# A ViT block on one core: values weighed in three fp16 passes, with the exps' terms cast in halves

## The chip, the cores and the metric

The kernel runs on one core of a Trainium2 chip. The metric is the device time of one execution in microseconds (us), the median of three runs. TensorE does matmuls (PE in the profile, its weight loads PEld), VectorE is DVE, ScalarE ACT, GpSimd POOL; SyncE (SP) issues the DMAs.

## The reference, cut to what matters

Eight batches of 512 tokens go through a tokenizer product, an attention block with 16 heads of 16 columns and a mixture of eight experts with sigmoid gates:

```python
h = einsum('bhid,oi,od->bho', x, weighted_sum, weight)      # [8, 512, 256]
h = h + attn(layernorm(h)); h = h + ffn(layernorm(h))
# attn: qkv = tokens @ qkv_w.T + qkv_b; q, k rotated and scaled to unit length
scores = einsum('bhqd,bhkd->bhqk', q, k) * 16 ** -0.5
out = einsum('bhqk,bhkd->bhqd', softmax(scores), v)         # then @ out_w.T + out_b
# ffn, for each of 8 experts: relu(x @ W1[e] + b1[e]) @ W2[e] + b2[e], times its gate, all summed
```

## The kernel before, in words

Everything is in fp32 quality; where matmuls are fp16, both operands are split in a high and a low fp16 half and three products are summed (high x high, high x low, low x high).

The FFN of one batch is 64 chunks, 8 for each expert. A chunk's first step (`f1`) is 6 matmuls into `bank_h`, then on ScalarE two Relus (`h32` in fp32 and `hh`, the high half, L724 and L727), then on GpSimd the low half `hl` (L616). Three chunks later comes its second step (`f2`), 12 matmuls into `bank_f`; after 8 chunks VectorE adds the expert's result (`acc`, L1150).

The attention of batch b+1 runs between the FFN chunks of batch b. `attention_order` gives each attention step a place, in chunks from the FFN's start, and `merge` writes one list of all steps. Every engine walks that same list, and each does its own part of a step, with semaphores between them; so the list sets the order on all engines. ScalarE alone first passes the list through `exps_first`, which swaps an `f1` with a `scores` step that directly follows it, so that the exp comes ahead of the chunk's Relus:

```python
for k in range(len(order) - 1):
    if order[k][0] == "f1" and order[k + 1][0] == "scores":
        order[k], order[k + 1] = order[k + 1], order[k]
```

A scores phase has 16 units (`UNITS`: 4 groups of heads x 4 tiles of keys) of two halves. Half n is a step `scores n`, `PACE` = 0.66 chunk after the one before, from 25.6 on: two row-tiled fp16 matmuls of 512 columns into `bank_s` (L820), then on ScalarE one exp of 128x1024 into `probs` (L693). There is one pair of score banks, so `scores n` waits on TensorE for exp n-1. The step `weigh u`, three paces after the unit's first scores, multiplies the unit's four heads with the values `v1` into `bank_o`: four fp32 matmuls in four column tiles of 32 (L834; the profile records two a matmul). `v1` has for each head 16 columns of values and 16 of ones, which give the sum of the exps. `probs` has two buffers, so an exp of unit u waits for the weighing of unit u-2. After four units come `out_copy` and `out_turn` (transposes, a reciprocal and a product, L1073 and L1076), and after all of them the projection, the second layernorm, the gates (`gates_turn`, L884, and a copy on ScalarE) and the bias matmuls (`bias2`, L891).

Batch 0's attention has no FFN beside it. Beside batch 0's FFN run batch 1's attention and the preparation of the experts: for each, VectorE takes maxima of the raw weights (`maxima`, L1163), computes scales (`scales`, L1194 to L1210) after a DMA round trip, and splits the weights in halves in four parts (`parts`: the high half on ScalarE, L739, the low on VectorE, L1174). In batches 1 to 7 the FFN loads the split weights from memory.

A `qkv` step adds the bias into `qk` and `v1` on VectorE (L1025, L1026); `rotate` then uses `tmp_b`, `tmp_a` (GpSimd, L623) and ScalarE's squares.

## Time and profile before

| | us |
|---|---|
| median of 3 runs | 1947.99 (1947.15 to 1950.42) |
| the profiled execution, its span | 1948.63, 1946.8 |
| TensorE busy | 1840.2 (95%) |
| ScalarE busy | 1070.7 (55%) |
| VectorE busy | 753.6 (39%) |
| GpSimd busy | 661.6 (34%) |

The profile is of one execution. Busy is the union of an engine's instructions; start-to-start times are shorter than durations, as neighbours overlap by some 0.1 us. "Idle before" names the engine that ended the wait. The mean granted TensorE clock is 0.98 of full speed; it is lower in parts of the first 130 us and around 200 to 250 us.

### The profile page before, as it was taken

Reading aid. Unit: us, or ns where it says so; the run is one execution under the profiler, and the core shown is the slowest. Engines: PE = TensorE matmul, PEld = TensorE weight load, DVE = VectorE, ACT = ScalarE, POOL = GpSimd, SP = SyncE. Lnnn points to the kernel's source line nnn. Section 1 sums busy time; section 2 is a strip of 40 time slices with the busy share of each in tenths; the row PEclk is TensorE's granted clock in tenths of the full one; section 3 lists DMA queues with packets and bytes.
Section 4 is the critical chain, followed back from the end, with each engine's and each line's share of the span. In section 5 each row is a group of like instructions: output and inputs, shape, how many; then the busy total and the mean of one; then the engine's idle time right before and its main releaser. Section 6 shows DMA issues by size and latency. Waiting matters only on the chain.

```text
span 1946.8 us, 31769 instructions
## 1 busy us (share of the span) xinstructions
PE 1840.2 (95%) x12608; PEld 1163.8 (60%) x12608; DVE 753.6 (39%) x1600; ACT 1070.7 (55%) x1645; POOL 661.6 (34%) x559
## 2 busy tenths in 40 slices
PE   5469799999999999999999999999999999999999
PEld 4137444676457754677546764577645775466666
DVE  7866744546014540246213470044601454021001
ACT  2544477545764466554665456644565546655444
POOL 1003422334233342334323343233423334234443
PEclk9689899999999999999999999999999999999999
DMA  4421543434123151231513333133412314122221
GB/s 161 130 98 39 149 144 132 159 120 109 65 81 128 64 130 66 87 120 66 130 66 109 98 91 105 63 112 98 124 52 106 114 66 114 65 87 98 109 91 52
DMA packets 109780, 194.55 MB, mean 100 GB/s; under 512 B 72616, under 2 KB 86464, under 8 KB 93248
## 3 DMA queue, kind: packets, MB, share of 16 engines
q1 hardware_dynamic: 109632, 192.51, 30.6%
q8 instruction: 100, 1.64, 0.3%
q14 instruction: 48, 0.39, 0.1%
HBM read 154.73 MB, written 20.98 MB: 90 GB/s over the span
## 4 chain that ended last, share of the span: by engine, by line
PE 77%; DVE 8%; DMA 4%; ACT 3%; issue 3%; SPq 0%; DVEq 0%; ACTq 0%
PE bank_h L908 28%; PE bank_f L927 10%; PE bank_f L930 9%; PE bank_f L929 9%; PE bank_o L834 5%; PE bank_s L820 4%; PE bank_s L750 3%; PE bank_s L751 3%; PE bank_s L752 3%; DMA kt<-probs 1%; DMA kt<-stack 1%; DVE tmp_b L1038 1%; DVE acc L1150 1%; DMA raw<-in_w_dram 1%; DVE y L948 1%
## 5 line engine op out<-in xcount | busy, mean ns | idle before, releaser
L616 POOL TENSOR_TENSOR hl<-h,hh 128x512 f16<-128x512 f32 x512 | 600.4, 1173 | 1159.6 <-ACT hh L727 722.7
L908 PE MATMUL bank_h<-x,w1s 128*128 128x512 f16 x3072 | 752.5, 382 | 7.6 <-ACT hh L727 7.2
L724 ACT ACTIVATE h<-bank_h,b1s 128x512 f32<-128x512 f32 x512 | 351.3, 686 | 467.0 <-PE bank_h L908 466.9
L927 PE MATMUL bank_f<-w2s,hh 128*128 128x256 f16 x2048 | 561.4, 274 | 14.2 <-DVE acc L1150 14.2
L929 PE MATMUL bank_f<-w2s,hh 128*128 128x256 f16 x2048 | 559.6, 273 | 0.0
L930 PE MATMUL bank_f<-w2s,hl 128*128 128x256 f16 x2048 | 559.5, 273 | 0.0
L908 PEld LDWEIGHTS bank_h<-x,w1s 128*128 128x128 f16 x3072 | 287.8, 99 | 335.5 <-issue 45.6
L727 ACT ACTIVATE hh<-bank_h,b1s 128x512 f16<-128x512 f32 x512 | 350.0, 684 | 0.0
L693 ACT ACTIVATE probs<-bank_s 128x1024 f32<-128x1024 f32 x240 | 246.5, 1027 | 175.3 <-PE bank_s L820 174.2
L927 PEld LDWEIGHTS bank_f<-w2s,hh 128*128 128x128 f16 x2048 | 201.7, 98 | 123.2 <-issue 58.0
L1150 DVE SCALAR_TENSOR_TENSOR acc<-bank_f,gw,acc 128x256 f32<-128x256 f32 x256 | 106.1, 477 | 367.8 <-PE bank_f L930 367.5
L929 PEld LDWEIGHTS bank_f<-w2s,hh 128*128 128x128 f16 x2048 | 201.0, 98 | 50.8 <-issue 0.2
L930 PEld LDWEIGHTS bank_f<-w2s,hl 128*128 128x128 f16 x2048 | 200.9, 98 | 23.8
L1073 DVE RECIPROCAL rc<-bank_m 128x16 f32<-128x16 f32 x32 | 8.2, 257 | 379.1 <-PE bank_m L844 379.1
L834 PE MATMUL bank_o<-probs,v 128*32 128x512 f32 x1024 | 138.1, 612 | 1.0 <-ACT tmp_b L648 0.6
L820 PE MATMUL bank_s<-qt,kt 64*128 64x512 f16 x480 | 94.7, 391 | 35.7 <-DMA kt<-probs 25.8
L820 PEld LDWEIGHTS bank_s<-qt,kt 64*128 64x128 f16 x480 | 23.2, 93 | 120.5 <-issue 78.4
L750 PE MATMUL bank_s<-mix,xh 128*128 128x256 f32 x240 | 71.6, 298 | 16.6 <-DVE xl L971 16.6
L971 DVE TENSOR_TENSOR xl<-xraw,xh 128x512 fp32r<-128x512 f32 x58 | 41.9, 732 | 76.1 <-ACT xh L648 63.0
L752 PE MATMUL bank_s<-mix,xl 128*128 128x256 f32 x240 | 68.5, 285 | 0.0
L751 PE MATMUL bank_s<-mix,xh 128*128 128x256 f32 x240 | 68.3, 284 | 0.0
L623 POOL TENSOR_TENSOR tmp_a<-qk,cos 128x512 f32<-128x512 f32 x32 | 40.8, 1276 | 78.2 <-DVE qk L1025 78.2
(157 smaller groups left out, 1520.0 us busy)
## 6 DMA issues: line engine op xcount, KB each, us to landing
w1s<-w_parts SPq DMA_DIRECT2D x56, 1024.0 KB, 4.8
w2s<-w_parts SPq DMA_DIRECT2D x56, 1024.0 KB, 4.8
raw<-in_w_dram SPq DMA_DIRECT2D x16, 1024.0 KB, 6.6
xraw<-in_x_t_dram SPq DMA_DIRECT2D x30, 512.0 KB, 4.8
w_parts<-w1s SPq DMA_DIRECT2D x8, 1024.0 KB, 8.7
w_parts<-w2s SPq DMA_DIRECT2D x8, 1024.0 KB, 11.4
out_dram<-acc SPq DMA_DIRECT2D x16, 256.0 KB, 6.0
turned_gates<-maxima_rows SPq DMA_DIRECT2D x6, 192.0 KB, 3.5
```

What stands on the lines that cost most here:

```text
L616: pool.tensor_tensor(hl[n % HBUFS][:], h32[n % 2][:], hh[n % HBUFS][:], ALU.subtract)\
L693: act.activation(probs[u % 2][:, 2 * half:2 * half + 2, :], score_banks(n, fb is None)[:, :, :], ACT.Exp, scale=SCORE_SCALE).then_inc(expe ...
L724: act.activation(h32[n % 2][:], bank_h[n % 2][:, :], ACT.Relu, bias=b1s[:, e, m:m + 1]).then_inc(h_hi.sem, 1)
L727: act.activation(hh[n % HBUFS][:], bank_h[n % 2][:, :], ACT.Relu, bias=b1s[:, e, m:m + 1]).then_inc(h_hi.sem, 1)
L750: pe.matmul(out_ap, high[k], w[k], start=start and k == 0, stop=False, skip_group_check=True)
L752: last = pe.matmul(out_ap, low[k], w[k], start=False, stop=stop and k == n - 1, skip_group_check=True)
L820: pe.matmul(score_banks(n, fb is None)[:, j, :], kt[lo:lo + 64, h // 2, tile * P:(tile + 1) * P], qt[lo:lo + 64, h // 2, :], start=True, s ...
L834: last = pe.matmul(bank_o[32 * j:32 * j + 32, :], v1[:, tile, h, :, :].rearrange("p s d -> p (s d)"), probs[n % 2][:, j, :], start=(tile = ...
L908: last = pe.matmul(bank_h[n % 2][:, :], w[:, wp, k, m * P:(m + 1) * P], x16s[fb % 2][:, xp, k, :], start=(k == 0 and wp + xp == 0), stop=( ...
L927: pe.matmul(o, high, w[:, 0, m, :], start=(m == 0 and t % 2 == 0), stop=False, skip_group_check=True)
L929: pe.matmul(o, high, w[:, 1, m, :], start=False, stop=False, skip_group_check=True)
L930: last = pe.matmul(o, low, w[:, 0, m, :], start=False, stop=(m == HM - 1), skip_group_check=True)
```

## The change

Batch 0's attention is computed as before. From batch 1 on:

- The values are kept in fp16 as a high and a low half (`v16`, in the bytes of the old `v1`, which is now `v32`). A weighing is three passes of four column-tiled fp16 matmuls (v high x p high, v low x p high, v high x p low) instead of one of fp32.
- The exps write fp32 terms into `exps`, two buffers in `qk`, which is free by then, and wait only for the subtraction that last read that buffer. A new step `halves n`, 0.8 pace behind `scores n`, casts them into halves in the bytes of `probs`: the high half of even n on ScalarE right behind the exp, that of odd n on VectorE, the low half of both by a subtraction on VectorE. These casts wait for the weighing of unit u-2.
- `weigh` comes one pace later (four paces after its unit's first scores), and with it `out_copy`, `out_turn` and everything behind (`behind` = 1).
- On `qkv`, v goes through `tmp_b`: bias added, cast, subtraction; the rotation waits for that.
- Once, the largest value of v's weights is found (`v_max`: a VectorE reduction and a GpSimd reduction across partitions), and after batch 0's attention VectorE scales the v part of `qkvw` and `qkvb` by a power of two and `outw` back (`v_scaled`; GpSimd writes the ones and zeros of `v16`).

```diff
-    first = 25.6
+    first, behind = 25.6, 0 if alone else 1
     for n in range(2 * UNITS):
-        steps.append((first + PACE * n, "scores", n))
+        steps += [(first + PACE * n, "scores", n), (first + PACE * (n + 0.8), "halves", n)]
     for u in range(UNITS):
-        steps.append((first + PACE * min(2 * u + 3, 2 * UNITS) + 1e-6, "weigh", u))
+        steps.append((first + PACE * min(2 * u + 3 + behind, 2 * UNITS + behind) + 1e-6, "weigh", u))
...
-    prep = []
+    prep = [(3.4, "v_scaled", 0)]
...
+        halves = [p[:].rearrange("p j t -> p (j t)").bitcast(F16).rearrange("p (s j t) -> p s j t", s=2, j=4)
+                  for p in probs]
+        exps = [qk[:, 2 * i:2 * i + 2, :] for i in range(2)]
...
                 elif stage == "scores":
                     u, half = divmod(n, 2)
-                    if half == 0:
+                    if half == 0 and ab == 0:
                         wait(act, weighed, ab, u - 1)
                     wait(act, scored, ab, 2 * n + 2)
+                    if ab == 0:
+                        terms = probs[u % 2][:, 2 * half:2 * half + 2, :]
+                    else:
+                        wait(act, qk_unit, ab, TT)
+                        wait(act, halved, ab - 1, n - 1)
+                        terms = exps[n % 2]
+                    act.activation(terms, score_banks(n, fb is None)[:, :, :], ACT.Exp, scale=SCORE_SCALE)\
+                       .then_inc(exped.sem, 1)
+                    if ab and half == 0:
+                        wait(act, exped, ab, n + 1)
+                        wait(act, weighed, ab, u - 1)
+                        copy(halves[u % 2][:, 0, 0:2, :], terms).then_inc(high_even.sem, 1)
...
                 elif stage == "weigh":
                     g, tile = divmod(n, TT)
...
+                    if ab == 0:
+                        passes = [(v32[:, tile], probs[n % 2])]
+                    else:
+                        v_high, v_low = v16[:, 0, tile], v16[:, 1, tile]
+                        p_high, p_low = halves[n % 2][:, 0], halves[n % 2][:, 1]
+                        passes = [(v_high, p_high), (v_low, p_high), (v_high, p_low)]
+                    for k, (v, p) in enumerate(passes):
+                        for j in range(4):
+                            last = pe.matmul(bank_o[32 * j:32 * j + 32, :],
+                                             v[:, 4 * g + j].rearrange("p s d -> p (s d)"), p[:, j, :],
+                                             start=(tile == 0 and k == 0),
+                                             stop=(tile == TT - 1 and k == len(passes) - 1), skip_group_check=True)
...
+                    values = tmp_b[:, 0:D]
+                    wait(dve, summed, ab, n)
+                    half_v.link(dve, dve.tensor_tensor(values, at_v[:, 0:D], qkvb[:, 2 * D:QKV], ALU.add))
+                    values = values.rearrange("p (h d) -> p h d", d=HD)
+                    half_v.link(dve, dve.tensor_copy(v16[:, 0, n, :, 0, :], values))
+                    dve.tensor_tensor(v16[:, 1, n, :, 0, :], values, v16[:, 0, n, :, 0, :], ALU.subtract)\
+                       .then_inc(qkv_out.sem, 1)
...
+                elif stage == "halves":
+                    u, half = divmod(n, 2)
+                    high, low = (halves[u % 2][:, part, 2 * half:2 * half + 2, :] for part in range(2))
+                    wait(dve, weighed, ab, u - 1)
+                    if half:
+                        wait(dve, exped, ab, n + 1)
+                        half_v.link(dve, dve.tensor_copy(high, exps[n % 2]))
+                    else:
+                        wait(dve, high_even, ab - 1, u + 1)
+                    dve.tensor_tensor(low, exps[n % 2], high, ALU.subtract).then_inc(halved.sem, 1)
```

ScalarE, from the first scores of batch 2 on, before (an exp is `probs<-bank_s`, a chunk's Relus are `h` and `hh`):

```order
L693 ACTIVATE probs<-bank_s 128x1024 x2
L724 ACTIVATE h_0<-bank_h,b1s 128x512
L727 ACTIVATE hh<-bank_h,b1s 128x512
L693 ACTIVATE probs<-bank_s 128x1024
L724 ACTIVATE h_1<-bank_h,b1s 128x512
L727 ACTIVATE hh<-bank_h,b1s 128x512
L693 ACTIVATE probs<-bank_s 128x1024 x2
```

The same place now (an exp is `qk<-bank_s`, the cast of an even half `probs<-qk`):

```order
L721 ACTIVATE qk<-bank_s 128x1024
L670 ACTIVATE probs<-qk 128x1024
L756 ACTIVATE h_0<-bank_h,b1s 128x512
L759 ACTIVATE hh<-bank_h,b1s 128x512
L721 ACTIVATE qk<-bank_s 128x1024 x2
L670 ACTIVATE probs<-qk 128x1024
L756 ACTIVATE h_1<-bank_h,b1s 128x512
L759 ACTIVATE hh<-bank_h,b1s 128x512
L721 ACTIVATE qk<-bank_s 128x1024
L756 ACTIVATE h_0<-bank_h,b1s 128x512
L759 ACTIVATE hh<-bank_h,b1s 128x512
L721 ACTIVATE qk<-bank_s 128x1024
```

The second exp stood ahead of the first chunk's Relus and now stands behind them; so does the fifth, which was one of a pair.

VectorE in batch 1's scores, from one pair of scale computations on, before (`scl`, `unscale`, `b1s` end a scale computation, `w1s`, `w2s` are parts, `mx` maxima):

```order
L1207 TENSOR_SCALAR scl<-inv 128x2
L1208 SCALAR_TENSOR_TENSOR unscale<-pow 128x1
L1210 TENSOR_SCALAR b1s<-b1raw,scl 128x8
L1174 SCALAR_TENSOR_TENSOR w1s<-raw,scl,w1s 128x1024 x2
L1174 SCALAR_TENSOR_TENSOR w2s<-raw,scl,w2s 128x1024
L1073 RECIPROCAL rc<-bank_m 128x16
L1076 TENSOR_TENSOR normed<-bank_m,rc 128x4x64
L1174 SCALAR_TENSOR_TENSOR w2s<-raw,scl,w2s 128x1024
```

The same place now (`probs<-qk` casts, `probs<-qk,probs` subtractions):

```order
L1303 TENSOR_SCALAR b1s<-b1raw,scl 128x8
L1133 CAST probs<-qk 128x1024
L1136 TENSOR_TENSOR probs<-qk,probs 128x1024
L1243 SCALAR_TENSOR_TENSOR w1s<-raw,scl,w1s 128x1024
L1136 TENSOR_TENSOR probs<-qk,probs 128x1024
L1243 SCALAR_TENSOR_TENSOR w1s<-raw,scl,w1s 128x1024
L1133 CAST probs<-qk 128x1024
L1136 TENSOR_TENSOR probs<-qk,probs 128x1024
L1243 SCALAR_TENSOR_TENSOR w2s<-raw,scl,w2s 128x1024
L1136 TENSOR_TENSOR probs<-qk,probs 128x1024
L1243 SCALAR_TENSOR_TENSOR w2s<-raw,scl,w2s 128x1024
```

Between the parts of an expert there is now a halves step each.

TensorE at the gates of batch 1, before (`wg` the gates' transposes, `b2sb` the bias matmuls):

```order
L884 MATMUL bank_m<-ident,wg 24x128 x4
L927 MATMUL bank_f<-w2s,hh 128x256
L929 MATMUL bank_f<-w2s,hh 128x256
L930 MATMUL bank_f<-w2s,hl 128x256
```

There the twelve matmuls of an f2 chunk follow, and then the bias matmuls. Now:

```order
L972 MATMUL bank_f<-w2s,hh 128x256
L974 MATMUL bank_f<-w2s,hh 128x256
L975 MATMUL bank_f<-w2s,hl 128x256
L929 MATMUL bank_m<-ident,wg 24x128 x4
L936 MATMUL bank_s<-b2sb,turned_gates 128x256 x4
```

The f2 chunk stands ahead of both, and the bias matmuls come directly behind the transposes.

## Rows read from the trace of the kernel before

**Rows 1.** The page: busy time by engine; the chain that ended last.
```profile
PE 1840.2 (95%) x12608; PEld 1163.8 (60%) x12608; DVE 753.6 (39%) x1600; ACT 1070.7 (55%) x1645; POOL 661.6 (34%) x559
...
PE 77%; DVE 8%; DMA 4%; ACT 3%; issue 3%; SPq 0%; DVEq 0%; ACTq 0%
```

**Rows 2.** Busy us (instructions) by engine, TensorE clock, DMA, in two windows.
```profile
240.00:335.00 95.00, 90.04 (x588) 42.39 (x589) 40.92 (x67) 70.08 (x89) 24.33 (x21) 0.97 0.42 139
...
710.00:805.00 95.00, 95.00 (x645) 47.28 (x644) 7.03 (x18) 63.70 (x87) 32.08 (x27) 1.00 0.24 79
```

**Rows 3.** Timeline, TensorE, batch 3's scores: start us, us, engine, line, what, count.
```profile
715.07 0.39 PE L820 MATMUL bank_s<-qt,kt 64*128 64x512 f16 x2
...
748.51 0.16 PEld L834 LDWEIGHTS bank_o<-probs,v 128*32 128x32 f32 x8 [0.23 <-issue]
...
748.51 1.07 PE L834 MATMUL bank_o<-probs,v 128*32 128x512 f32 x8
...
749.51 0.28 PE L927 MATMUL bank_f<-w2s,hh 128*128 128x256 f16 x1
...
750.92 0.39 PE L820 MATMUL bank_s<-qt,kt 64*128 64x512 f16 x2
...
751.25 1.47 PE L908 MATMUL bank_h<-x,w1s 128*128 128x512 f16 x6
...
752.55 0.27 PE L927 MATMUL bank_f<-w2s,hh 128*128 128x256 f16 x1
...
799.77 0.64 PE L834 MATMUL bank_o<-probs,v 128*32 128x512 f32 x4
```

**Rows 4.** Timeline, ScalarE, the same stretch.
```profile
749.57 0.68 ACT L724 ACTIVATE h<-bank_h,b1s 128x512 f32<-128x512 f32 x1
...
750.14 0.69 ACT L727 ACTIVATE hh<-bank_h,b1s 128x512 f16<-128x512 f32 x1
...
751.44 1.02 ACT L693 ACTIVATE probs<-bank_s 128x1024 f32<-128x1024 f32 x1 [0.61 <-PE bank_s L820]
...
752.75 0.69 ACT L724 ACTIVATE h<-bank_h,b1s 128x512 f32<-128x512 f32 x1 [0.29 <-PE bank_h L908]
```

**Rows 5.** ScalarE by line and shape: count | busy us, mean ns | idle before.
```profile
L648 ACT ACTIVATE mix<-probs 128x1024 fp32r<-128x1024 f32 x2 | 2.1, 1056 | 7.2 <-DVE probs L464 7.2
```

**Rows 6.** VectorE by line and shape.
```profile
L1174 DVE SCALAR_TENSOR_TENSOR w1s<-raw,scl,w1s 128x1024 f16<-128x1024 f32 x16 | 20.5, 1282 | 18.2 <-ACT w1s L739 18.0
...
L1172 DVE TENSOR_SCALAR w1s<-raw,scl 128x1024 f16<-128x1024 f32 x4 | 3.0, 748 | 0.0
...
L1076 DVE TENSOR_TENSOR normed<-bank_m,rc 128x256 f32<-128x256 f32 x32 | 13.6, 424 | 1.1
```

**Rows 7.** Timeline, VectorE and GpSimd, batch 3's rotations.
```profile
674.44 0.69 DVE L1043 TENSOR_TENSOR qk<-tmp_a,tmp_b 128x512 f32<-128x512 f32 x1
...
680.67 1.16 POOL L616 TENSOR_TENSOR hl<-h,hh 128x512 f16<-128x512 f32 x1 [0.61 <-PE bank_f L930]
...
680.71 1.66 DVE L1043 TENSOR_TENSOR qk<-tmp_a,tmp_b 128x512 f32<-128x512 f32 x1
```

**Rows 8.** Timeline, TensorE, three places.
```profile
135.47 0.57 PE L891 MATMUL bank_s<-b2sb,turned_gates 24*128 24x256 f32 x1 [0.68 <-ACT turned_gates L648]
...
332.71 0.64 PE L834 MATMUL bank_o<-probs,v 128*32 128x512 f32 x4
...
695.57 0.27 PE L927 MATMUL bank_f<-w2s,hh 128*128 128x256 f16 x1 [1.14 <-DVE acc L1150]
```

**Rows 9.** Timeline, VectorE, start of batch 1's scores.
```profile
245.25 2.29 DVE L1163 TENSOR_REDUCE mx<-raw 128x1 f32<-128x2048 f32 x1 [9.06 <-DMA raw<-in_w_dram]
...
247.72 1.66 DVE L1150 SCALAR_TENSOR_TENSOR acc<-bank_f,gw,acc 128x256 f32<-128x256 f32 x4
...
255.67 0.68 DVE L1194 TENSOR_REDUCE mxr<-turned_gates 128x3 f32<-128x384 f32 x1 [6.30 <-DMA turned_gates<-maxima_rows]
...
257.97 0.23 DVE L1210 TENSOR_SCALAR b1s<-b1raw,scl 128x8 f32<-128x8 f32 x1
```

More of the change, by code:

```diff
@@ L131, in merge @@
         return order
-    between = {("scores", 0): [("maxima", 0), ("maxima", 1), ("reduce", 0), ("scales", 0),
+    between = {("scores", 0): [("v_max", 0), ("maxima", 0), ("maxima", 1), ("reduce", 0), ("scales", 0),
                                ("parts", 0), ("parts", 1), ("parts", 2), ("parts", 3)],
@@ L140, in bodies @@
     first = []
-    for step in attention_order(alone=True):
+    for step in [s for s in attention_order(alone=True) if s[1] != "halves"]:
         first += [step[1:]] + between.get(step[1:], [])
@@ L823, in steps @@
                     g, tile = divmod(n, TT)
-                    wait(pe, exped, ab, 2 * (n + 1))
+                    if ab == 0:
+                        wait(pe, exped, ab, 2 * (n + 1))
+                    else:
+                        wait(pe, halved, ab - 1, 2 * (n + 1))
+                    if n == 0 and ab == 1:
+                        pe.wait_ge(pool_consts, 2)
                     if n == 0:
@@ L831, in steps @@
                         wait(pe, o_out, ab, g)
-                    for j in range(4):
-                        h = 4 * g + j
-                        last = pe.matmul(bank_o[32 * j:32 * j + 32, :],
-                                         v1[:, tile, h, :, :].rearrange("p s d -> p (s d)"),
-                                         probs[n % 2][:, j, :], start=(tile == 0), stop=(tile == TT - 1),
-                                         skip_group_check=True)
+                    if ab == 0:
+                        passes = [(v32[:, tile], probs[n % 2])]
[9 more added lines that the diff above has]
+                                             stop=(tile == TT - 1 and k == len(passes) - 1), skip_group_check=True)
                     last.then_inc(weighed.sem, 1)
@@ L1174, in steps, with scale_values @@
                     dve.scalar_tensor_tensor(low, cut, scale, high, ALU.mult, ALU.subtract).then_inc(parts_lo, 1)
+            def scale_values():
+                link = scale_v.link
+                b_v = qkvb[:, 2 * D:QKV]
+                dve.wait_ge(v_max_all, 1)
+                dve.tensor_reduce(vbound[:, 1:2], b_v, AX.X, ALU.max, apply_absolute_value=True)
+                link(dve, dve.tensor_tensor(vbound[:, 0:1], vmxr[:, 0:1], vmxr[:, 1:2], ALU.max))
+                link(dve, dve.scalar_tensor_tensor(vbound[:, 0:1], vbound[:, 0:1], float(D), vbound[:, 1:2],
+                                                   ALU.mult, ALU.add))
+                link(dve, dve.tensor_scalar(vbound[:, 0:1], vbound[:, 0:1], FLOOR, None, ALU.max))
+                link(dve, dve.tensor_scalar(vbound[:, 0:1].bitcast(I32), vbound[:, 0:1].bitcast(I32), EXPONENT, None,
+                                            ALU.bitwise_and))
+                link(dve, dve.tensor_scalar(vbound[:, 1:2].bitcast(I32), vbound[:, 0:1].bitcast(I32), -1.0,
+                                            float(2 * ONE_BITS), ALU.mult, ALU.add))
+                dve.tensor_scalar(vscl[:, 1:2], vbound[:, 0:1], 1.0 / TOP, None, ALU.mult)
+                link(dve, dve.tensor_scalar(vscl[:, 0:1], vbound[:, 1:2], TOP, None, ALU.mult))
+                wait(dve, projected, 0, TT)
+                for part in range(2):
+                    w_v, w_o = qkvw[:, part, :, 2 * D:QKV], outw[:, part]
+                    dve.tensor_scalar(w_v, w_v.bitcast(F32), vscl[:, 0:1], None, ALU.mult)
+                    dve.tensor_scalar(w_o, w_o.bitcast(F32), vscl[:, 1:2], None, ALU.mult)
+                dve.tensor_scalar(b_v, b_v, vscl[:, 0:1], None, ALU.mult).then_inc(v_scaled, 1)
+                dve.wait_ge(v_scaled, 1)
             def stack_b2():
```

47 lines of the change are left out of this document (37 added, 10 removed).

## The prediction

> **What bounds the kernel now.** I read the page first, then busy times by window, then one scores stretch as a timeline of TensorE and of ScalarE, then VectorE in the stretch where expert weights are still being split. The page shows TensorE busy 95% of the span and 77% of the chain that ended last; the other engines are busy 34 to 55% [rows 1]. By window the kernel has two kinds of scores phase (32 score steps and 16 weighings of one batch, beside the FFN of the batch before). In batches 2 to 7 TensorE has no idle time (95.00 of 95 us), VectorE works 7 us of 95 and ScalarE 64. In batch 1, whose scores run beside the FFN of batch 0, VectorE already works 41 us of 95, since it splits the raw weights there, and ScalarE 70 [rows 2]. So an operation on VectorE is nearly free in six phases and dear in one.
>
> **The weighing.** One weighing holds TensorE 1.00 us, from its start to that of the next instruction, 748.51 to 749.51 [rows 3]; the records are eight, two for each fp32 matmul, four column tiles at a time. The change makes it three fp16 passes of four tiles in the 112 weighings of batches 1 to 7. No row shows a 32-column fp16 pass. Nearest: six FFN matmuls of 512 fp16 columns followed by an FFN matmul of another kind take 1.30 us (751.25 to 752.55), so 0.22 each; a score step, one pass of two row tiles, takes 0.33 (750.92 to 751.25), so a change of tiling adds about 0.11 [rows 3]. That gives 0.11 + 3 x 0.22 = 0.77; if each pass stood alone, 3 x 0.33 = 0.99; if the change of tiling overlapped by a third, 0.73. I take 0.78, near the first, since the fp32 row has the same four tiles overlapping. Gain: 0.22 us a weighing, 3.5 a batch, 24.6 in all; bounds 1 and 30.
>
> The loads of the second four tiles are done by 748.67 (0.16 us from 748.51) while the first four still compute [rows 3]. The Trainium skill, TensorE: Matmul & The Clock Gate, section Part 3 (packing small matmuls), has it that weight loads overlap running matmuls only where the row group differs, and column tiles share theirs. By that rule each pass would show its load and the weighing would cost about the 0.99 above, leaving a gain of 1 us in place of 24.6; the row is against it.
>
> **ScalarE in the scores phase.** It gains one copy of 128x1024 to fp16 for each even half. A row of that size from SBUF is 1.06 us [rows 5], about 0.95 from start to start. The copy waits for the end of its own exp, so an even half costs 1.02 + 0.04 + 0.95 = 2.0 us where it was 0.92. The FFN's two Relus of a chunk occupy 1.14 (749.57 to 750.14 is one, 0.57) [rows 4]. Per unit (two halves, 1.32 chunks): 2.0 + 0.92 + 1.5 + 0.12 for the output copy = 4.5 us, against TensorE's two score steps, a weighing, 1.32 chunks of 1.30 + 1.35 and its share of the output transposes: 0.64 + 0.78 + 3.50 + 0.13 = 5.0. It fits, with little room, and here the order matters. Before, exps_first swaps an exp ahead of the Relus of the chunk just before it. The new "halves" step stands between "f1" and "scores" in the list, so most swaps no longer happen: the exp is now queued behind Relus whose matmuls end only as its own scores start. TensorE's next score step needs that exp, since there is one pair of score banks.
>
> I walked the phase with these figures (exp 0.51 us after its scores start, Relus 1.50 after their matmuls start, an f2 chunk before a score step 1.41, an f1 chunk 1.40 [rows 3, 4]). One stretch of it, in us from score step 8: step 12 stands at 11.07, its exp at 11.58 to 12.60, the copy to 13.58. TensorE goes on with the weighing, the output transposes and f1 of chunk 34 at 12.67, so the Relus run from 14.17 to 15.31. Step 13 comes at 14.07; its exp is ready at 14.58 but runs from 15.31 to 16.33. Step 14 would come 0.32 + 1.41 after step 13, at 15.80, and starts at 16.38. Over the phase TensorE stalls before score step 2 (1.3 us), 8 (0.6), 14 (0.6), 18 (0.1), 20 (0.6) and 24 (0.5): 3.7 us. Before there was none: the 85.7 us from step 0 to the end of weighing 15 (715.07 to 799.77, and 1.0) [rows 3] are what the pieces add up to. So the 3.5 us are given back, +0.2 a batch. The last weighing now needs VectorE's last cast and subtraction 3.7 us after its scores; +0.1.
>
> **VectorE in batches 2 to 7.** Each unit gains two subtractions of 128x1024 with two SBUF inputs and one cast. Nearest rows: L1174, some 1.28 us, and L1172, 0.75 [rows 6]; 3.3 us of 5.0, where little else runs. But an instruction with two SBUF inputs waits while GpSimd runs: the 0.69 us L1043 took 1.66 when a GpSimd subtraction had started 0.04 us ahead of it [rows 7]. The halves have a pace (2.4 us) to spare before the exp that reuses their buffer, which covers one such wait; I cost it at 0, and as a rival below.
>
> **Smaller places, once a batch.** (a) All attention steps behind the weighing come one pace (0.66 chunk) later. That takes away the f2 chunk between the transposes of the gates and the bias matmuls. In batch 0 they already stand side by side: 0.68 us idle on top of the transposes [rows 8]. The TensorE clock is full here in the later batches (1.00 in the scores window [rows 2]); I take 0.8, for the copy and its latencies. (b) With v, VectorE gains a cast and a subtraction of 256 columns before each rotation (0.6 to 0.8 us together, a quarter of rows 6 and a start each). After tile 3 its queue is unbroken up to the acc of expert 1, for which TensorE already waits 1.1 us [rows 8]; 0 to 0.85 of it comes through, partly absorbed by GpSimd's turns; I take 0.4. Sum with the 0.3 above: 1.5 us a batch.
>
> **VectorE in batch 1.** Between the first and the last halves step its list holds 3 accs (1.7 each), 3 scale computations (2.5, 255.67 to 258.2), 11 subtractions of weight parts (1.28), 2 pairs of maxima (4.6), 3 output turns (0.42 and a reciprocal, 0.7) by [rows 6, 9]: 37.9 us. The halves add 32 x 1.28 + 16 x 0.78 = 53.4. Together 91.3. The first halves step stands behind the maxima that end at 247.5, after a 9.06 us wait for a DMA [rows 9]. 247.5 + 91.3 = 338.8, with VectorE never idle. The last weighing ended at 333.7 before (332.71 [rows 8] and 1.0), and 1.4 us of FFN that came after it now come ahead: 335.1. So at least +4 us. On top: each part waits for ScalarE's copy, which is now queued behind exps that wait for halves; by a walk of one expert's period about 1 us a period, 3 in all; and 59 instructions take the port that GpSimd holds a quarter of the time (24.3 of 95 us [rows 2]), 0.15 us each, 9 in all. +16, bounds +4 and +27 (0.3 us a conflict, 6 us of waits). Scores, exps and weighings follow VectorE and TensorE is in order, so all of this lands on the end.
>
> **The rest.** Scaling v's weights is some 12 VectorE instructions, 4 to 5 us by the durations of rows 6 and 9, near the start of batch 1's steps, where VectorE still waits for other engines and a DMA; 0 to 3 us of it can come through, I take 1. The maximum of the v weights (0.7 us) and the two GpSimd memsets lie where those engines wait: 0.
>
> **Sum.** Seven batches x 1.5 for the once-a-batch places and the phase's balance, without the 0.2 + 0.1 in batch 1 which the +16 replaces: 6 x 1.5 + 1.2 = 10.2. With 16 and 1: +27.2. Before, the profiled execution took 1948.6 us (span 1946.8), the median 1948.0; so 1976.
>
> **Rivals.**
> Other side, faster (23%): TensorE stays the sole bound in batches 2 to 7, because a score step finds its exp done in spite of the lost swaps. The deciding point is ScalarE's backlog when an exp becomes ready: below 0.2 us at the short gaps (0.32 + 1.41 us) there is no stall. For it: ScalarE has 31 us free in 95 [rows 2] and needs 15. Against: the exp behind two Relus has 1.14 us of backlog by construction. Then 6 x (-3.5 + 1.3) = -13.2, batch 1 at its minimum +4 + 1.2 + 1: -7, so 1942; with 0.73 for the weighing 5 less, 1937.
> VectorE keeps up in batch 1 (12%): its DMA and ScalarE waits of before are all filled, no port conflicts show, +4; the stalls stay. 1948.6 + 10.2 + 5 = 1964.
> The port decides everywhere (13%): 3.3 us of VectorE and 1.32 x 1.16 of GpSimd are 4.8 us a unit of 5.0; if they exclude each other wholly and an exp waits one more GpSimd instruction every fourth unit, that is 4 x 1.2 us a batch: 1976 + 29 = 2005. For it: rows 7. Against: both have slack of a pace or a chunk.
> The change not doing what it says (fp16 passes that cost 0.99): 1976 + 6 x 1 at most, since the stalls shrink as the weighing grows; inside the range, no own chance.
>
> The Trainium skill, FP8 and Floating Point Precision, section TensorE Precision Notes, has fp32 as four passes through the array, so that three fp16 passes would be three quarters of it: 112 weighings of 1.00 us x 1/4 = 28 us less by that estimate, against my 24.6. As a rule for the whole kernel it gives 1921, which holds only if nothing but TensorE counts; I give that 2% within the faster rival, since rows 2 show the other engines' load.
>
> **How the numbers follow.** My forecast has 52%, the rivals 23, 12 and 13. Likeliest time 1976, its own range 1960 to 1990. Eight times in ten: 1940 to 1996, which leaves out the far ends of the faster rival and most of the port's. Within 0.2% (3.9 us, about what a measurement of this kernel can tell) is reached only between cases: 4%. Faster 24%, slower 72%.
>
> **What would show it.** In the changed profile: the weighing near 0.78 us from start to next; TensorE idle before scores released by ScalarE's exps, 3 to 4 us a batch in batches 2 to 7; the last weighing of batch 1 some 15 us later than the 332.71 of before [rows 8], with VectorE above 90% busy ahead of it; the bias matmuls released by ScalarE's copy, 7 times some 0.8 us; VectorE's subtractions mostly at 1.28 with some above 2. Wrong would be: scores phases of batches 2 to 7 some 3 us shorter than the 85.7 from step 0 to the end of weighing 15 [rows 3], or batch 1 with VectorE idle while TensorE works.

## The result, and the profile after

The changed kernel takes 1970.55 us (median of 4 runs, 1969.12 to 1971.10) against 1947.70 us before (4 runs, 1947.15 to 1950.42): ratio 1.0108, 95% interval 1.0096 to 1.0121. It is slower by 1.1%. The profiled execution has a span of 1967.2 us, 20.4 more than before.

The page of the changed kernel, busy time by engine and the chain that ended last; both answer to [rows 1]:

```profile
PE 1823.4 (93%) x13056; PEld 1173.3 (60%) x13056; DVE 1144.3 (58%) x2006; ACT 1182.5 (60%) x1757; POOL 710.4 (36%) x562
...
PE 69%; DVE 10%; ACT 6%; issue 5%; DMA 4%; SPq 0%; ACTq 0%; DVEq 0%
```

TensorE has less to do and a smaller share of the chain; VectorE's busy time rose by 391 us. Where the time went shows in the starts of the f1 chunks, which cut the execution into the periods of the eight FFNs. The first f1 matmul of FFN 0 started at 125.14 us before and starts at 124.88 now; that of FFN 1 started at 395.94 and starts at 410.33:

```profile
124.88 0.59 PE L953 MATMUL bank_h<-x,w1s 128*128 128x512 f16 x1
...
410.33 0.38 PE L953 MATMUL bank_h<-x,w1s 128*128 128x512 f16 x1
```

So FFN 0's period, which carries batch 1's attention, went from 270.80 to 285.45 us (+14.65). Cut the same way, the periods of FFNs 1 to 6 sum to 1379.98 before and 1385.98 now (+1.0 each), FFN 7 has 170.89 and 170.88, and the start is 0.26 earlier. That is the 20.4. FFN 0's 14.65 in turn are 3.37 ahead of batch 1's first score step (118.46 where it was 115.09), 8.93 from the first to the last score step (98.69, was 89.76) and 2.35 behind it (68.30, was 65.96).

The windows that answer to [rows 2] (us, then busy us and instructions of TensorE, its weight loads, VectorE, ScalarE, GpSimd, granted clock, DMA share, GB/s), one in batch 1's scores and one in batch 3's:

```profile
243.00:343.00 100.00, 84.15 (x616) 42.71 (x617) 86.04 (x110) 83.05 (x101) 28.26 (x20) 0.97 0.37 122
725.50:820.50 95.00, 91.60 (x706) 48.21 (x707) 59.07 (x66) 79.59 (x102) 38.83 (x27) 1.00 0.25 81
```

TensorE, which had no idle time in batch 3, now has 3.4 us; in batch 1 VectorE is busy 86 of 100 us where it was 41 of 95. What TensorE waits for over the whole kernel (us in total, times, longest):

```profile
PE bank_s L854 <- ACT qk L721: 31.1, 42, 2.4
...
PE bank_s L936 <- ACT turned_gates L670: 5.4, 8, 0.7
...
PE bank_s L782 <- DVE v L1084: 3.3, 2, 2.7
...
PE bank_o L879 <- DVE probs L1136: 2.8, 1, 2.8
```

L854 are the scores, L936 the bias matmuls, L782 the qkv matmuls, L879 the weighing. The first row was 4.5 us before, the second one place of 0.7.

**The weighing.** A timeline of the changed kernel, one weighing of batch 3, TensorE's loads (PEld) and matmuls:

```profile
740.76 0.34 PEld L879 LDWEIGHTS bank_o<-probs,v 128*32 128x32 f16 x12 [0.23 <-issue]
740.76 0.83 PE L879 MATMUL bank_o<-probs,v 128*32 128x512 f16 x12
...
741.52 0.28 PE L972 MATMUL bank_f<-w2s,hh 128*128 128x256 f16 x1
```

From its start to the next instruction it takes 0.764 us (median of 96 in batches 2 to 7) where it took 0.998. The twelve loads are done in 0.34 us beneath the matmuls. The Trainium skill, TensorE: Matmul & The Clock Gate, Part 3 (packing small matmuls), lets loads overlap running matmuls only where the row group differs; the 0.99 that the prediction worked out for that case did not come.

**The steady phase.** Batch 3's first and last score step of the changed kernel, and its one long stall, on TensorE's timeline:

```profile
730.99 0.39 PE L854 MATMUL bank_s<-qt,kt 64*128 64x512 f16 x2
...
732.72 0.39 PE L854 MATMUL bank_s<-qt,kt 64*128 64x512 f16 x2
...
735.68 0.39 PE L854 MATMUL bank_s<-qt,kt 64*128 64x512 f16 x2 [1.16 <-ACT qk L721]
...
813.34 0.39 PE L854 MATMUL bank_s<-qt,kt 64*128 64x512 f16 x2
```

82.35 us from first to last score step, where it was 81.97 (715.07 in [rows 3], and 797.04 for the last). Inside lie 14 weighings, so 14 x 0.234 = 3.3 us less work; 78.7 would be left, and 3.65 are lost. TensorE's waits before score steps add up to 3.2 of them; the other 0.4 is not accounted for. ScalarE's timeline of the same moment shows how:

```profile
732.51 1.06 ACT L670 ACTIVATE probs<-qk 128x1024 f16<-128x1024 f32 x1
733.47 0.67 ACT L756 ACTIVATE h<-bank_h,b1s 128x512 f32<-128x512 f32 x1
734.04 0.68 ACT L759 ACTIVATE hh<-bank_h,b1s 128x512 f16<-128x512 f32 x1
734.61 1.02 ACT L721 ACTIVATE qk<-bank_s 128x1024 f32<-128x1024 f32 x1
```

The exp of score step 1 (scores at 732.72) starts only at 734.61, behind the copy of the even half and both Relus, and TensorE's step 2 waits for it.

**Batch 1.** VectorE by line, from its first low half to the end of the phase (count | busy us, mean ns | idle before and its releaser):

```profile
L1136 DVE TENSOR_TENSOR probs<-qk,probs 128x1024 f16<-128x1024 f32 x31 | 40.2, 1311 | 0.5
...
L1133 DVE CAST probs<-qk 128x1024 f16<-128x1024 f32 x15 | 10.8, 718 | 1.6 <-ACT qk L721 1.6
L1243 DVE SCALAR_TENSOR_TENSOR w1s<-raw,scl,w1s 128x1024 f16<-128x1024 f32 x6 | 7.8, 1304 | 3.1 <-ACT w1s L771 3.1
L1243 DVE SCALAR_TENSOR_TENSOR w2s<-raw,scl,w2s 128x1024 f16<-128x1024 f32 x5 | 6.7, 1337 | 1.7 <-ACT w2s L771 1.7
```

And the last weighing of batch 1 on TensorE's timeline, which answers to the 332.71 of [rows 8]:

```profile
348.77 0.60 PE L879 MATMUL bank_o<-probs,v 128*32 128x512 f16 x5 [2.77 <-DVE probs L1136]
```

It is 16.1 us later and waits for VectorE.

The 3.37 us ahead of the scores are not waits of TensorE. From FFN 0's first f1 to batch 1's first score step, before and now:

```profile
125.14:240.23 115.09, 94.13 (x594) 64.47 (x595) 80.61 (x146) 53.74 (x86) 40.64 (x31) 0.92 0.29 78
```

```profile
124.88:243.34 118.46, 97.49 (x593) 66.36 (x594) 87.72 (x167) 53.88 (x86) 43.39 (x33) 0.90 0.28 76
```

The idle time is 21.0 us in both; TensorE is busy 3.36 us longer with the same work, at a lower mean granted clock (0.90 for 0.92). One such stretch is new. TensorE waits 2.7 us for the halves of v, and then the granted clock is at its lower level (1.2 GHz) for 3.4 us; before, the wait at that place was 1.2 us, and the clock stayed full (1.00 in 190 to 194). Its timeline and the window behind the wait:

```profile
190.35 0.76 PE L782 MATMUL bank_s<-qkvw,turned_h 128*128 128x512 f32 x1 [2.70 <-DVE v L1084]
```

```profile
190.30:193.70 3.40, 3.35 (x10) 2.80 (x11) 3.37 (x5) 1.07 (x3) 1.58 (x1) 0.51 0.00 0
```

### The profile page after: what moved, and what is told of

Read it like the earlier page. It is cut to its first block, busy times and chain, and to the rows that moved or that the text cites. A ratio compares the mean times of both kernels' runs of the same rounds, so it can differ in the third digit from the quotient of the medians.

```text
span 1967.2 us, 33635 instructions
## 1 busy us (share of the span) xinstructions
PE 1823.4 (93%) x13056; PEld 1173.3 (60%) x13056; DVE 1144.3 (58%) x2006; ACT 1182.5 (60%) x1757; POOL 710.4 (36%) x562
## 4 chain that ended last, share of the span: by engine, by line
PE 69%; DVE 10%; ACT 6%; issue 5%; DMA 4%; SPq 0%; ACTq 0%; DVEq 0%
PE bank_h L953 26%; PE bank_f L972 9%; PE bank_f L974 8%; PE bank_f L975 8%; PE bank_o L879 3%; PE bank_s L782 3%; ACT qk L721 3%; PE bank_s L783 3%; PE bank_s L784 3%; PE bank_s L854 3%; ACT hh L759 1%; DVE probs L1136 1%; DMA kt<-stack 1%; DMA kt<-probs 1%; DVE acc L1217 1%
## 5 line engine op out<-in xcount | busy, mean ns | idle before, releaser
L631 POOL TENSOR_TENSOR hl<-h,hh 128x512 f16<-128x512 f32 x512 | 646.7, 1263 | 1131.0 <-ACT hh L759 688.1
L1136 DVE TENSOR_TENSOR probs<-qk,probs 128x1024 f16<-128x1024 f32 x224 | 276.9, 1240 | 126.3 <-ACT probs L670 122.2
L759 ACT ACTIVATE hh<-bank_h,b1s 128x512 f16<-128x512 f32 x512 | 348.7, 681 | 0.0
L721 ACT ACTIVATE qk<-bank_s 128x1024 f32<-128x1024 f32 x224 | 229.3, 1024 | 64.1 <-PE bank_s L854 52.5
L854 PE MATMUL bank_s<-qt,kt 64*128 64x512 f16 x480 | 94.2, 389 | 60.4 <-ACT qk L721 31.1
L1133 DVE CAST probs<-qk 128x1024 f16<-128x1024 f32 x112 | 94.3, 842 | 56.3 <-ACT qk L721 56.3
L670 ACT ACTIVATE probs<-qk 128x1024 f16<-128x1024 f32 x112 | 118.4, 1057 | 3.6
L879 PE MATMUL bank_o<-probs,v 128*32 128x512 f16 (+1 forms) x1472 | 111.7, 406 | 3.8 <-DVE probs L1136 2.8
L854 PEld LDWEIGHTS bank_s<-qt,kt 64*128 64x128 f16 x480 | 23.0, 92 | 145.6 <-ACT qk L721 71.0
L782 PE MATMUL bank_s<-mix,xh 128*128 128x256 f32 x240 | 71.6, 298 | 16.7 <-DVE xl L1016 16.6
```

The lines of the kernel that those rows point to most:

```text
L631: pool.tensor_tensor(hl[n % HBUFS][:], h32[n % 2][:], hh[n % HBUFS][:], ALU.subtract)\
L721: act.activation(terms, score_banks(n, fb is None)[:, :, :], ACT.Exp, scale=SCORE_SCALE)\
L759: act.activation(hh[n % HBUFS][:], bank_h[n % 2][:, :], ACT.Relu, bias=b1s[:, e, m:m + 1]).then_inc(h_hi.sem, 1)
L782: pe.matmul(out_ap, high[k], w[k], start=start and k == 0, stop=False, skip_group_check=True)
L854: pe.matmul(score_banks(n, fb is None)[:, j, :], kt[lo:lo + 64, h // 2, tile * P:(tile + 1) * P], qt[lo:lo + 64, h // 2, :], start=True, s ...
L879: last = pe.matmul(bank_o[32 * j:32 * j + 32, :], v[:, 4 * g + j].rearrange("p s d -> p (s d)"), p[:, j, :], start=(tile == 0 and k == 0), ...
```

## The experiments

All are made from the changed kernel and named as in their expectations (e1, e2, ...). Durations called a phase run from a batch's first score step to its last. A ratio is to runs of the kernel before, taken beside that experiment (medians 1947.98 to 1948.64).

**e1: exps ahead of the Relus again.**

```diff
 def exps_first(order):
-    order = list(order)
+    order = [step for step in order if step[0] != "halves"]
```

> ScalarE's list looks past the halves steps, so that an exp again runs ahead of the Relus of the chunk that precedes it; nothing else changes. Theory (an exp waits behind two Relus): TensorE's idle time before scores in batches 2 to 7 (31.1 us in the whole changed kernel, of which 12.2 in batch 1 and 4.5 in batch 0 were there or have another cause) goes to below 0.5 us a batch, and each of the six batches gets 3 to 4 us shorter: 1970.5 - 6 x 3.5 = 1949.5, so no different from the kernel before. Batch 1 moves by less than 2 us, since VectorE sets it. Rival (TensorE's wait comes from something else, such as the even halves' copy alone or VectorE's halves): 1968 to 1971, and the idle time before scores stays at 3 us a batch. Second rival (the Relus are now late and f2 waits for them): the idle time moves to the FFN matmuls, 1960 or more.

Measured: 1958.46 us (5 runs), ratio to before 1.0051 (1.0039 to 1.0064), 12 us less than the changed kernel where 21 were expected. TensorE's timeline, batch 3, first and last score step:

```profile
729.29 0.39 PE L854 MATMUL bank_s<-qt,kt 64*128 64x512 f16 x2
...
809.78 0.39 PE L854 MATMUL bank_s<-qt,kt 64*128 64x512 f16 x2
```

80.49 us, 1.85 less. ScalarE's timeline there: the exp of step 1 now comes ahead of the Relus, but still behind the copy.

```profile
730.80 1.06 ACT L670 ACTIVATE probs<-qk 128x1024 f16<-128x1024 f32 x1
731.77 1.01 ACT L721 ACTIVATE qk<-bank_s 128x1024 f32<-128x1024 f32 x1
732.67 0.68 ACT L756 ACTIVATE h<-bank_h,b1s 128x512 f32<-128x512 f32 x1
```

The lost swaps are shown as half of the 3.65 us. The first theory named them as the whole; 1.8 us stayed, 1.4 of it in short waits before score steps 4 (0.52), 18 (0.41), 24 (0.41) and 30 (0.09). The periods of FFNs 1 to 6 are 10.5 us shorter in sum, and FFN 0's is 2.0 shorter.

**e8: all casts of halves on VectorE in batches 2 to 7, on top of e1.**

```diff
-                    if ab and half == 0:
+                    if ab == 1 and half == 0:
...
-                    if half:
+                    if half or ab > 1:
                         wait(dve, exped, ab, n + 1)
```

> As e1_swap, and in batches 2 to 7 VectorE also casts the even halves, so that ScalarE has no copy left in the scores steps there. In e1_swap the stretch from the first to the last score step was still 80.49 us, 1.8 above what its pieces add up to (81.97 of before less 14 weighings x 0.234 = 78.7). Theory (the rest is ScalarE's copy of the even half, 0.96 us from start to start, which stands ahead of the next exp): 78.7, so 6 x 1.8 = 10.8 less than the 1958.5 of e1_swap: 1947.6. Rival (VectorE now has some 4.2 us of casts and subtractions in a unit of 5.0 and stays behind, above all where GpSimd holds it up, so that exps wait for halves): 80.5 or more, 1958 to 1970.

Measured: 1953.88 us (11 runs), ratio 1.0027 (1.0018 to 1.0036), 4.6 us less than e1 where 10.8 were expected. Batch 3's phase on TensorE's timeline, and the window of [rows 2]:

```profile
727.57 0.39 PE L854 MATMUL bank_s<-qt,kt 64*128 64x512 f16 x2
...
807.36 0.39 PE L854 MATMUL bank_s<-qt,kt 64*128 64x512 f16 x2
```

```profile
725.50:820.50 95.00, 94.21 (x728) 50.25 (x727) 81.52 (x84) 63.46 (x87) 34.54 (x27) 1.00 0.23 80
```

79.79 us: the copy accounts for 0.7 of the 1.8. Of the last 1.1 us, 0.8 are TensorE's waits before score steps 4, 5, 8 and 18; 0.3 is not accounted for. Before steps 4, 5 and 8 (0.7 us) the exp that the step needs had itself waited for VectorE, which is busy 81.5 of 95 us now. Ten of the phase's 32 exps wait for it, as the rival had said. The lines show GpSimd, VectorE and ScalarE:

```profile
740.17 1.16 POOL L631 TENSOR_TENSOR hl<-h,hh 128x512 f16<-128x512 f32 x1 [4.18 <-ACT hh L759]
740.31 2.11 DVE L1136 TENSOR_TENSOR probs<-qk,probs 128x1024 f16<-128x1024 f32 x1
...
745.37 1.02 ACT L721 ACTIVATE qk<-bank_s 128x1024 f32<-128x1024 f32 x1 [1.81 <-DVE probs L1136]
```

A low half that starts while a GpSimd instruction runs takes 2.10 us in the mean (84 of the 192 in batches 2 to 7), any other 1.23 at most. In the changed kernel none of the 192 took more than 1.23.

**e4: a fourth pass in the weighing.**

```diff
+                        if ab > 1:
+                            passes.append((v_low, p_low))
```

> The weighing gets a fourth fp16 pass (low half of v by low half of the exps) in batches 2 to 7: 96 times a pass of some 0.22 us, 20.9 us of TensorE's work, 14 of 16 in a batch between its first and last score step. Theory (that stretch holds 3.6 us of idle time in which TensorE waits for ScalarE's exps, and a longer weighing moves the next score step later and so fills it): the stretch of 82.35 us grows by 0 to 1 us, the two weighings behind it by 0.4: +3 to +9 us, 1973 to 1979. Rival (TensorE is the bound and every us of it counts): +20.9, 1991.

Measured: 1988.33 us (4 runs), 17.8 more than the changed kernel, where 3 to 9 were expected and 20.9 by the rival. The theory fell. What TensorE waits for in batch 3's phase, first in the changed kernel, then in this one:

```profile
PE bank_s L854 <- ACT qk L721: 3.2, 5, 1.2
```

```profile
PE bank_s L854 <- ACT qk L721: 2.9, 5, 1.1
```

A weighing takes 0.980 us (0.216 for the pass); the phase grew by 2.7 of 14 x 0.216 = 3.0 us, and the waits are the same five. The order on TensorE's timeline says why: before score step 2 no weighing has run yet, and before steps 8, 14 and 20 the weighing stands ahead of the f1 chunk whose Relus the exp waits behind. There a longer weighing moves the Relus and the exp by the same amount as the score step that waits, and the waits are 0.53 us in both kernels. Only before step 24 does the wait shrink, from 0.41 to 0.18. A wait that a queue order makes is not slack.

**e3: bias matmuls one f2 chunk later.**

```diff
             else:
-                while waiting:
+                while waiting and waiting[0][0] < c + 0.5:
                     order.append(waiting.pop(0)[1:])
```

> The bias matmuls stand one f2 chunk (1.3 us) later in every batch with an FFN beside it; the transposes of the gates stay. Theory: TensorE's wait of 0.68 us for ScalarE's copy of the transposed gates goes in seven places, 7 x 0.7 = 4.9: 1965.6. Rival (the next thing is late instead: the first mix of the coming batch or the first f1 needs VectorE's bias additions, now 1.3 us later): no gain, 1970 to 1971, with a new wait of 0.5 us or more behind the bias matmuls.

Measured: 1964.93 us (median of 5 runs; four lie between 1964.24 and 1966.12, and one took 3704.04, for which nothing on record has a cause), 5.6 less than the changed kernel, where 4.9 were expected. From the last score step to the next FFN's first f1 batches 2 to 7 take 59.38 us instead of 60.13, six times 0.75; batch 1, where more varies, takes 67.07 instead of 68.30. No wait before the bias matmuls is left in batches 1 to 7.

**e6: batch 1 as before.** The fp32 weighing, its buffers and its order are kept for batch 1; `v_scaled` moves to the first steps of batch 2.

```diff
-                    if ab == 0:
+                    if ab < 2:
                         passes = [(v32[:, tile], probs[n % 2])]
...
-    return first, merge(attention + prep, done=2), merge(attention), merge([])
+    return (first, merge(kept + prep, done=2), merge(attention + [(3.4, "v_scaled", 0)]), merge(attention),
+            merge([]))
```

> Batch 1 keeps the fp32 weighing and its order of before; the three fp16 passes start with batch 2, and the scaling of v's weights moves to the start of batch 2's steps. Theory: the FFN period of batch 0, 14.65 us longer after the change, goes back to what it was, less 0 to 1 us for the maxima; batch 2's period gains 0.3 to 1 us for the scaling: 1970.5 - 14 = 1956.5 (1955 to 1958). Rival (part of the 14.65 us is carried in from the stretches before, so that it stays): 1960 or more. Second rival (the scaling costs as much in batch 2, since TensorE has no idle time there to hide it): 1959 to 1961.

Measured: 1953.03 us (8 runs), ratio 1.0026 (1.0016 to 1.0036), 17.5 less than the changed kernel where 14 were expected. FFN 0's period is 270.62 us (126.35 to 396.97), what it was before, and batch 2's is no longer than in the changed kernel (230.76 against 231.11), so the scaling of v's weights costs nothing there. The granted clock in 190 to 194 is 1.00 again. By the spans the gain is 15.1 us, of which 14.8 is this period; the medians show 2.4 more, which lies within their spread. Batch 1 is three quarters of the loss.

**What sets batch 1's pace: VectorE relieved, both relieved, ScalarE relieved.** Three kernels, in batch 1 alone: e2, the subtraction of the low half on 8 of 512 columns; e9, that and the even halves cast on VectorE instead of ScalarE; e11, ScalarE's copy on 8 of 512 columns.

```diff
-                        passes = [(v_high, p_high), (v_low, p_high), (v_high, p_low)]
+                        passes = [(v_high, p_high), (v_low, p_high), (v_high, p_high if ab == 1 else p_low)]
...
-                    dve.tensor_tensor(low, exps[n % 2], high, ALU.subtract).then_inc(halved.sem, 1)
+                    cut = 8 if ab == 1 else TOKENS
+                    dve.tensor_tensor(low[:, :, 0:cut], exps[n % 2][:, :, 0:cut], high[:, :, 0:cut], ALU.subtract)\
+                       .then_inc(halved.sem, 1)
```

> In batch 1 alone VectorE's subtraction of the low half of the exps covers 8 of 512 columns (about 0.1 us for 1.31), and the third pass of the weighing reads the high half, so TensorE's work is the same and the low half of batch 1's exps is left out of the result. Theory (VectorE sets the pace of batch 1's scores): 32 x 1.2 = 38 us of VectorE's time go, and the scores phase of batch 1, 98.7 us from the first score step to the last, gets back to the 90 us of before less what the steady batches show, so 7 to 10 us less: 1961 to 1963. Rival (batch 1 is slowed by ScalarE, whose copies of weight parts, exps and even halves queue up): less than 3 us less, 1968 to 1970.

```diff
-                    if ab and half == 0:
+                    if ab > 1 and half == 0:
...
-                    if half:
+                    if half or ab == 1:
                         wait(dve, exped, ab, n + 1)
...
```

> As e2_low_sliver (batch 1 subtracts 8 columns of 512 and leaves the low half of its exps out), and in batch 1 VectorE instead of ScalarE casts the even halves. In e2_low_sliver the stretch from first to last score step of batch 1 was still 95.85 us, where TensorE's work is 89.76 - 3.3 = 86.5. Theory (with VectorE relieved, ScalarE is the next bound there: exps, copies of even halves, Relus and copies of weight parts; 16 x 0.96 = 15.4 us of its queue go): the stretch falls by 4 to 8 us to 88 to 92, the kernel to 1956 to 1960. Rival (the rest is the order of the exps behind Relus and weight parts alone, or VectorE's scale computations and maxima): less than 2 us, 1962 to 1964.

```diff
-                        copy(halves[u % 2][:, 0, 0:2, :], terms).then_inc(high_even.sem, 1)
+                        cut = 8 if ab == 1 else TOKENS
+                        copy(halves[u % 2][:, 0, 0:2, 0:cut], terms[:, :, 0:cut]).then_inc(high_even.sem, 1)
...
+                        if ab == 1:
+                            p_high, p_low = (part[:, 2:4] for part in (p_high, p_low))
...
```

> In batch 1 alone ScalarE's copy of the even half covers 8 of 512 columns, VectorE's subtraction for it takes the exps on both sides (same size), and the weighing reads the odd half's tiles twice, so TensorE and VectorE do the same work; batch 1's result lacks the even halves. In e9_b1_scalar both engines were relieved (period of FFN 0: 271.84 us), in e2_low_sliver VectorE alone (278.14), in the changed kernel none (285.45). Theory (VectorE sets batch 1's pace and ScalarE comes second, only once VectorE is relieved): less than 2 us less, 1968.5 to 1970.5. Rival (the two share it in turn, an exp waits for halves and halves wait for exps and copies, so each engine's relief pays by itself): 3 to 7 us less, 1963 to 1967.

| relieved in batch 1 | median us | FFN 0's period | of it, from the first score step on |
|---|---|---|---|
| none (the changed kernel) | 1970.55 | 285.45 | 166.99 |
| ScalarE (e11) | 1969.32 | 285.45 | 164.77 |
| VectorE (e2) | 1964.08 | 278.14 | 160.10 |
| both (e9) | 1956.49 | 271.84 | 153.28 |

e11 and e9 fell within their expected ranges; e2 brought 6.5 us where 7 to 10 were expected. In e11's window of batch 1's scores ScalarE's busy time falls from 83 to 70 us, VectorE's is 88 of 100:

```profile
243.00:343.00 100.00, 81.93 (x598) 41.10 (x599) 87.98 (x108) 69.58 (x100) 30.38 (x22) 0.95 0.39 126
```

e11's equal period hides a gain. Its stretch ahead of the scores, which the edit does not touch, took 120.68 us for 118.46, and TensorE ran there at its lower clock for longer. The window of 140 to 146, in the changed kernel and in e11:

```profile
140.00:146.00 6.00, 5.31 (x40) 4.49 (x41) 3.33 (x7) 2.51 (x5) 1.70 (x1) 1.00 0.30 90
```

```profile
140.00:146.00 6.00, 5.17 (x25) 5.15 (x26) 1.98 (x4) 1.17 (x2) 1.69 (x1) 0.52 0.28 90
```

So the last column is the one to compare. e4 and e12, which leave this stretch as it is, have 166.68 and 167.84 in it. ScalarE's relief alone is worth 2.2 us at most (1.2 by the medians, whose runs overlap), VectorE's alone 6.9, and once VectorE is relieved ScalarE's brings another 6.8. So VectorE is the main bound in batch 1, and ScalarE stands 7 us behind it.

**e12: the high half of v read from PSUM instead of cast.**

```diff
-                    half_v.link(dve, dve.tensor_copy(v16[:, 0, n, :, 0, :], values))
+                    half_v.link(dve, dve.tensor_tensor(v16[:, 0, n, :, 0, :], at_v[:, 0:D].rearrange("p (h d) -> p h d", d=HD),
+                                                       qkvb[:, 2 * D:QKV].rearrange("p (h d) -> p h d", d=HD),
+                                                       ALU.add))
```

> VectorE's cast of the v values to their high half, 1.13 us in all 28 places though the cast of a four times larger tile takes 0.69, is replaced by a second addition that reads PSUM and writes the fp16 half (the first addition took 0.41); the subtraction of the low half stays (0.43 now). Theory (the cast waits until GpSimd's product of q and k with the cosines, 1.28 us from 179.10, has ended): the wait moves to the subtraction behind it, which has two SBUF inputs and takes about 1.0 us instead of 0.43; the stretch from the first f1 of batch 0's FFN to batch 1's first score step, 118.46 us, gets less than 0.8 shorter, the kernel 1969 to 1971. Rival (the cast itself is slow, for its strided fp16 output): the subtraction stays at 0.43, the stretch loses 2 to 3 us, the kernel 1967 to 1968.

Measured: 1970.51 us (4 runs), no change. VectorE and GpSimd in the changed kernel, tile 0 of batch 1:

```profile
178.94 0.42 DVE L1081 TENSOR_TENSOR tmp_b<-bank_s,qkvb 128x256 f32<-128x256 f32 x1
...
179.10 1.28 POOL L638 TENSOR_TENSOR tmp_a<-qk,cos 128x512 f32<-128x512 f32 x1 [3.96 <-DVE qk L1073]
...
179.39 1.14 DVE L1083 CAST v<-tmp_b 128x256 f16<-128x256 f32 x1
...
180.57 0.42 DVE L1084 TENSOR_TENSOR v<-tmp_b,v 128x256 f16<-128x256 f32 x1
```

And in this one, where L1086 is the subtraction:

```profile
178.78 0.41 DVE L1081 TENSOR_TENSOR tmp_b<-bank_s,qkvb 128x256 f32<-128x256 f32 x1
...
178.94 1.28 POOL L638 TENSOR_TENSOR tmp_a<-qk,cos 128x512 f32<-128x512 f32 x1 [3.96 <-DVE qk L1073]
...
179.23 0.42 DVE L1083 TENSOR_TENSOR v<-bank_s,qkvb 128x256 f16<-128x256 f32 x1
179.69 0.82 DVE L1086 TENSOR_TENSOR v<-tmp_b,v 128x256 f16<-128x256 f32 x1
```

GpSimd's product ends at 180.38 and 180.22, and the first VectorE instruction that reads SBUF alone ends 0.15 and 0.29 us behind it. The instruction with an operand in PSUM was not held up (0.42). The wait moved on, and the stretch ahead of batch 1's scores lost 0.8 us of its 118.46 (117.65; it is 118.00 in e4, which does not change it, so this gain is hardly clear of what differs from run to run). The phase grew by 0.9: the period is 285.49. The Trainium skill, SBUF — State Buffer, section SBUF: two separate sides, has an exclusive lock on a port pair that VectorE and GpSimd share, held for a whole instruction; these rows agree with it.

**e10: what the runs point to, together.** Batch 1 as before; from batch 2 on the swaps, the later bias matmuls, and all casts of halves on VectorE. The diff is those of e1, e3, e6 and e8 together.

> All that the runs so far point to: batch 1 with the fp32 weighing and the order of before (17.5 us in e6_batch1_old), exps ahead of Relus again (1.85 us a batch in e1_swap) and all casts on VectorE (1.8 expected of e8_even_dve) in batches 2 to 7, bias matmuls an f2 chunk later in those (0.75 us a batch in e3_bias2_later). Sum: 1953.0 - 6 x (1.85 + 1.8 + 0.75) = 1926.6, 1.1% below the kernel before (ratio 0.989). If all casts on VectorE bring nothing: 1937.4 (0.9946). If VectorE falls behind with them: 1940 or more.

Measured: 1932.75 us (4 runs, 1930.20 to 1934.10), ratio to before 0.9917 (0.9904 to 0.9931), so faster than both kernels. Its page:

```profile
PE 1820.5 (94%) x12992; PEld 1168.7 (61%) x12992; DVE 1217.2 (63%) x2046; ACT 1065.7 (55%) x1645; POOL 679.5 (35%) x562
```

The 6.2 us missing against 1926.6 are the phase again: 79.78 us where 78.7 was counted on, six times 1.1.

## Why the prediction was right

The forecast was 1976 us with 72% on slower; the kernel takes 1970.6. The working gave +27.2 on the span, 9.0 of it in the six later batches and 18.2 in batch 1; the trace shows +20.4, with 6.0 and 14.65. Both parts came and each was smaller than said; the causes are those described, but for one: part of batch 1's loss is the clock.

- **Weighing, 0.78 and 0.22 less.** Measured 0.764 and 0.234 less. The addition of pieces (0.11 for the change of tiling and three passes at their column rate) held; 1.6 us of the total is this.
- **Steady stalls, 3.7 us a batch.** TensorE's waits are at the steps that the walk named: 1.16 us before step 2 (1.3 said), 0.53 before step 8 (0.6), 0.53 before 14, 0.05 before 18, 0.53 before 20, 0.41 before 24. They add up to 3.2; the phase loses 3.65, so its agreement with 3.7 includes 0.4 that the walk does not explain. The phase is +0.37 (+0.2 said). The reason given was too narrow: it named the lost swaps alone, and they are half. The walk itself had the copy of the even half in ScalarE's queue; the sentence above it did not.
- **"The stalls shrink as the weighing grows"**, used to bound the case of a slower pass at 6 us. Wrong: with a fourth pass they stayed at 2.9 us of 3.2, and 0.216 us a weighing cost 17.8 us. By an estimate from that, a weighing of 0.99 us instead of 0.78 would have cost some 17 us more, not 6, which is outside the forecast's own range. This is the one step whose mechanism failed, and it was not called upon; what follows are terms of a wrong size.
- **Bias matmuls, 0.8.** 0.68, seven times, and removed by one f2 chunk between.
- **VectorE's queue before the acc of expert 1, 0.4.** TensorE's wait there is 1.1 us as it was. The stretch ahead of the scores is 0.36 us longer in the mean of six batches, but it varies by over 1 us between them; this term is not settled.
- **Batch 1, +16.** The last weighing starts 16.1 us later, but that is not the same quantity: the +16 allowed for one f1 chunk (1.4 us) that now comes ahead of it, and for its end. On that count (335.1 to 349.5) it is 14.4 us. VectorE's list from its first halves step to its last took 98.1 us (250.60 to 348.7), 91.6 busy and 6.5 idle, where the prediction had 103 from 247.5. So the list was 5 too long: of the 9 us put on it for GpSimd's port, the 32 low halves show 3.5 (1335 ns in the mean over the whole batch, where the steady ones take 1225). And its start was put 3 too early (247.5 for 250.60): the whole phase began 3.1 us later than before (243.34 against 240.23), for the reason in the next point. That the two errors offset each other is luck.
- **Ahead of batch 1's scores, 0.4 + 1.** The prediction had 0.4 for the v casts and 1 for scaling v's weights; the stretch grew by 3.37. The v casts held up the qkv matmuls for 3.3 us at two places where it was 1.2 at one, and the granted clock fell behind the longer wait. The prediction had no term for the clock. The scaling cost nothing that shows: VectorE did it between 145.8 and 151.2, where it had waited 3.4 us for ScalarE, and moving it to batch 2 in e6 lengthened nothing.
- **The cast of v.** I gave cast and subtraction 0.6 to 0.8 us together; they take 1.55, since GpSimd's product starts 0.29 us ahead of the cast in all 28 places, released by VectorE's addition of q and k (L1073).

Against the rivals: TensorE as the sole bound (1942) failed on the stalls; VectorE keeping up (1964) is excluded by e2, in which relieving VectorE in batch 1 alone brings 6.5 us; the port everywhere (2005) did not come, as none of the steady low halves took more than 1227 ns.

## What to carry to other kernels

A helper that reorders by looking at neighbours in a list ("f1, then scores") breaks without a sign when a new kind of step is put between them: compare each engine's instruction order whenever a list gets a new entry. When work is moved off the busiest engine, price the one stretch where the receiving engine is already half full, and leave that stretch out of the change: here one batch of seven cost three quarters of the loss, and without that batch, with the exps' order mended, the bias matmuls later and ScalarE's copies moved, the same change gains 0.8%. A receiving engine has to be priced with what it waits for: here in e8, a VectorE subtraction that starts under a GpSimd instruction takes 2.10 us for 1.23. A wait that the order of a queue makes is not slack that other work can fill.

## What the runs showed of the hardware that was not expected

The wait of VectorE for GpSimd follows the operands: 28 of 28 casts of 256 columns from SBUF took 1.13 us beside GpSimd's product and ended 0.15 us behind it, longer than a cast of 1024 columns alone (0.69). In e12 an addition in the same place, with the same strided fp16 output but one operand in PSUM, took 0.42, and the SBUF subtraction behind it, the same operation type, went from 0.43 to 0.81. In e8 the split is complete: all 84 steady low halves that start under a GpSimd instruction are held up, none of the other 108.

It acts in the other direction too: GpSimd's subtraction of the Relu's halves has a mean of 1263 ns over its 512 places, where it was 1173 before the change. The 216 that start while a VectorE instruction without a PSUM input runs have a mean of 1409, the other 296 of 1157.
